# The mix of a four-layer network: head steps in another order, two operations on other engines, the next layer's first transfers in its tail

## What is computed

```python
x  = x + s * g                       # layer 1's result, then:
xn = layernorm(x)
# mixer of layer 2 (8 chunks of 2 sequences x 256 tokens, width 128):
h        = layernorm(xn) * ln_g + ln_b
xi, z    = split(h @ W_in)
xc       = silu(causal_conv4(xi) + conv_b)
dt, B, C = split(xc @ W_xp)
delta    = softplus(dt @ W_dt + dt_bias)
state_t  = state_{t-1} * exp(delta_t * A) + delta_t * xc_t * B_t     # 256 channels x 16 states
y        = sum_n(state * C) + xc * D_skip
s        = (y * silu(z)) @ W_out + xn
# gate of layer 2: 16 experts, 2 per token, 128 -> 512 -> 128 with relu
g        = silu(sum over the two experts of weight * (relu(xn @ W1 + b1) @ W2 + b2))
x        = x + s * g                 # layer 3 begins with this
```

## Time and profile before

| | us |
|---|---|
| median of 3 runs | 3733.08 (3729.55 to 3736.5) |
| the profiled execution | 3726.74 |
| its span, first to last instruction | 3725.0 |
| first to last scan of the mix (128 scans) | 1253.4 to 1972.7 |
| busy: PE 2920.9, DVE 2268.6, ACT 1773.6, POOL 1190.1 | |
| granted TensorE clock, mean over the span | 0.901 |

### The profile page before, as it was taken

One profiled execution on the slowest core, in us unless ns is written; L12 is line 12 of the kernel. 1 busy time (PEld: TensorE's weight loads), 2 busy tenths in 40 slices (PEclk: granted clock), 3 DMA queues, 4 the chain that ended last, 5 costly groups with the idle time before them and its releaser, 6 DMA issues. The chain is left out here.

```text
span 3725.0 us, 54922 instructions
## 1 busy us (share of the span) xinstructions
PE 2920.9 (78%) x20472; PEld 1596.2 (43%) x20580; DVE 2268.6 (61%) x3194; ACT 1773.6 (48%) x3989; POOL 1190.1 (32%) x854
## 2 busy tenths in 40 slices
PE   5887888888624788888876888888888888888887
PEld 3444444444323234444442444444544444444443
DVE  3444444544347678788784666675757656675755
ACT  2334333443223455555552554645555554645555
POOL 0000000000134355555453534343443534443432
PEclk9888998999855899999987999999999998999989
DMA  2000000000022233333231000000000000000000
GB/s 108 9 8 6 3 8 8 6 3 8 30 97 88 59 85 84 84 85 88 81 93 47 10 4 10 6 3 12 3 13 4 13 4 10 7 4 10 3 4 4
DMA packets 82485, 112.67 MB, mean 30 GB/s; under 512 B 9952, under 2 KB 47328, under 8 KB 81632
## 3 DMA queue, kind: packets, MB, share of 16 engines
q1 hardware_dynamic: 76896, 98.83, 8.8%
q0 software_dynamic: 5376, 11.02, 1.1%
HBM read 82.55 MB, written 27.26 MB: 29 GB/s over the span
## 5 line engine op out<-in xcount | busy, mean ns | idle before, releaser
L1470 POOL TENSOR_TENSOR l2m_ST<-l2m_ST,l_CT 128x1024 f32<-128x1024 f32 x128 | 316.3, 2471 | 353.0 <-DVE l2m_ST L1413 353.0
L394 ACT ACTIVATE l_PT<-PB 128x512 f32<-128x512 f32 x512 | 277.9, 595 | 315.8 <-PE PB L292 315.8
L1413 DVE TENSOR_TENSOR_SCAN l2m_ST<-l2m_DA,l2m_DB 128x1024 f32<-128x1024 f32 x128 | 354.0, 2766 | 4.4
L436 DVE TENSOR_REDUCE keep_MXP<-PB 128x4 f32<-128x1024 f32 x256 | 301.1, 1218 | 61.4 <-PE PB L265 61.4
L292 PE MATMUL PB<-l_QM,l_KP 32*128 32x256 f32 x2048 | 283.1, 394 | 55.7 <-ACT l_PT L394 55.7
L731 POOL MEMSET l_KV<- 128x4 f32 x8 | 0.8, 104 | 854.5 <-POOLq L109 854.5
L1868 POOL TENSOR_TENSOR l_PT<-l_PT,ahead_PEN 128x512 f32<-128x512 f32 x176 | 232.7, 1353 | 63.5 <-ACT l_PT L394 63.0
L292 PEld LDWEIGHTS PB<-l_QM,l_KP 32*128 32x128 f32 x2048 | 188.0, 188 | 134.4 <-ACT l_PT L394 87.8
L1407 DVE TENSOR_TENSOR l2m_DB<-PB,l_BT 128x1024 f32<-128x1024 f32 x128 | 155.4, 1214 | 139.5 <-PE PB L1252 139.3
L1358 ACT ACTIVATE l2m_DA<-PB,keep_aneg 128x510 f32<-128x510 f32 x256 | 161.0, 683 | 162.8 <-DVE l2m_ST L1413 89.4
L2063 ACT ACTIVATE l3f_PP<-PB,l3f_MN 128x128 f32<-128x128 f32 x512 | 180.8, 372 | 118.8 <-DVE l3f_MN L2129 118.8
(11 more groups left out here) (463 smaller groups left out, 6393.2 us busy)
## 6 DMA issues: line engine op xcount, KB each, us to landing
l2m_WB<-in_w2f_dram SPq DMA_DIRECT2D x80, 320.0 KB, 3.0
l2m_WB<-in_w2f_dram SPq DMA_DIRECT2D x80, 258.0 KB, 2.7
l2m_XR<-xs_mid SPq DMA_DIRECT2D x80, 64.0 KB, 1.8
ys_mid<-l2m_YO SPq DMA_DIRECT2D x80, 64.0 KB, 2.8
s_mid<-keep_S SPq DMA_DIRECT2D x18, 256.0 KB, 2.1
w3fs<-in_w3f_dram SPq DMA_DIRECT2D x1, 3127.0 KB, 18.6
x_mid<-keep_X SPq DMA_DIRECT2D x10, 256.0 KB, 3.0
keep_XI<-in_x_dram SPq DMA_DIRECT2D x9, 256.0 KB, 3.0
```

The costliest lines, as they stand in the source:

```text
L394: nc.scalar.activation(b.PT[:, u % slots].rearrange("p k q -> p (k q)"), PB[:, 4 + u % STBANKS, :], ACT.Exp).then_inc(s.exp_done, 1)
L436: nc.vector.tensor_reduce(dst[:, 2 * pair:2 * pair + 2, :, 16 + n % 2], PB[:, 2 * pair:2 * pair + 2, :].rearrange("p r (t k) -> p r t k", ...
L1413: nc.vector.tensor_tensor_scan(b.ST[:, g % RING].rearrange("p k t -> p (k t)"), b.DA[:, g % 2].rearrange("p k t -> p (k t)"), b.DB[:, g % ...
L1470: nc.gpsimd.tensor_tensor(b.ST[:, g % RING], b.ST[:, g % RING], b.CT[:, k % 2, :].unsqueeze(1).broadcast_to([128, 2, T]), ALU.mult).then_i ...
```

## The change

1. In the mix the projection moves from step 2 to step 3 on TensorE, and the sum with the input from step 3 to step 4 on VectorE (`add_input` stands behind that step's scan).
2. The head's steps 8 to 13 move one step later, to 9 to 14 (`head_step`). Step 8 has no head.
3. The affine step of the head's normalisation moves from VectorE (L927) to ScalarE. The subtraction L933 moves from VectorE to GpSimd, behind its multiplication of step 13, and VectorE's L934 waits for it; `drives` of the next chunk moves behind the multiplication of step 14. For chunk 0 the same happens at the end of the router's block.
4. The block behind the mix goes. SP issues its two loads ahead of the last sum's store. GpSimd copies the places at its start, and behind the last multiplication waits for all tile stores, issues two gathers, does the last gating, and issues the other six.

```diff
+    elif step == 2:
+        act.wait_ge(s.xm_scaled, k + 1)
+        XS = b.XM[:, :, TAPS - 1:]
+        nc.scalar.activation(XS, XS, ACT.Identity, scale=w.g, bias=w.b).then_inc(s.xm_ready, 1)
...
+def head_step(n):
+    return n if n < 8 else n - 1 if n > 8 else None
+
+
+def head_pool(nc, pool, s, b, k):
+    pool.wait_ge(s.dt_log, k + 1)
+    nc.gpsimd.tensor_tensor(b.EE[:], b.UU[:], b.EE[:], ALU.subtract).then_inc(s.error_taken, 1)
...
-        link(nc.vector.scalar_tensor_tensor(out=XS, in0=seq(PB[:, LANE, :]), scalar=-0.5, in1=seq(u), op0=ALU.mult, op1=ALU.mult))
-        nc.vector.tensor_scalar(XS, XS, w.g, w.b, ALU.mult, ALU.add).then_inc(s.xm_ready, 1)
+        nc.vector.scalar_tensor_tensor(out=XS, in0=seq(PB[:, LANE, :]), scalar=-0.5, in1=seq(u), op0=ALU.mult, op1=ALU.mult).then_inc(s.xm_scaled, 1)
...
     elif step == 13:
-        dve.wait_ge(s.dt_log, k + 1)
-        link(nc.vector.tensor_tensor(b.EE[:], b.UU[:], b.EE[:], ALU.subtract))
+        dve.wait_ge(s.error_taken, k + 1)
...
+                head_pool(nc, pool, mix, head, 0)
                 pool.wait_ge(s.scattered0, 16 * TT * CHUNKS)
...
                 store_tile(TILES - 1)
+                sp.wait_ge(s.s_stored, 16)
+                load_gated(nc, sp, c, 0, x_mid, s_mid, s.first_loaded)
                 store_sum(CHUNKS - 1)
+                sp.wait_ge(s.first_loaded, 32)
...
-                        if n == 2 and k:
+                        if n == 3 and k:
                             project(k - 1)
                         if k + 1 < CHUNKS:
-                            head_tensor(nc, pe, s, c, w, b, PB, k + 1, n)
+                            head_tensor(nc, pe, s, c, w, b, PB, k + 1, head_step(n))
...
-                        if k and n == 3:
+                        if k and n == 4:
                             add_input(k - 1)
...
+                nc.gpsimd.tensor_copy(r.places[:], r.idx[:, :, 0:TT]).then_inc(s.places_copied, 1)
                 drives(0)
...
                         if n == 13 and k + 1 < CHUNKS:
+                            head_pool(nc, pool, s, b, k + 1)
+                        if n == 14 and k + 1 < CHUNKS:
                             drives(k + 1)
+                rows = [(a, t) for a in range(2) for t in range(TT)]
+                pool.wait_ge(s.places_copied, 1)
+                pool.wait_ge(s.tile_stored0, 8 * TILES)
+                pool.wait_ge(s.tile_stored1, 8 * TILES)
+                for a, t in rows[:2]:
+                    gather_tile(nc, pool, c, r, ys_mid, a, t, s.gathered)
                 gated(CHUNKS - 1, 1)
-        clear(nc, s)
+                for a, t in rows[2:]:
+                    gather_tile(nc, pool, c, r, ys_mid, a, t, s.gathered)
+                pool.wait_ge(s.gathered, 32 * TT)
+        clear(nc, s, soft)
...
-        with ExitStack() as io:
-            s = record(**semaphores(nc, io, "first_loaded places_copied")._asdict(), gathered=soft.soft0)
-            with nc.Block() as block:
...
-                    load_gated(nc, sp, c, 0, x_mid, s_mid, s.first_loaded)
-                    sp.wait_ge(s.first_loaded, 32)
...
-                    gather_mixed(nc, pool, c, r2, ys_mid, s.gathered)
-                    pool.wait_ge(s.gathered, 32 * TT)
-            clear(nc, s, soft)
```

More of the change, by code:

```diff
@@ L778 @@
             "taps_ready xm_ready xz_ready z_copied conv_ready x_copied silu_x xd_ready bc_copied dt_ready dt_raw dt_u dt_error dt_log delta_ready drive_ready "
-            "b_spread b_copied c_spread c_copied pads_set gaps_set delta_spread drive_spread decay_ready drive_done state_ready part_ready y_added "
+            "b_spread b_copied c_spread c_copied pads_set gaps_set places_copied first_loaded xm_scaled error_taken delta_spread drive_spread decay_ready drive_done state_ready part_ready y_added "
             "y_taken y_gated mamba_ready s_added ")
@@ L1188, in layer2_route, with layer2_mix @@
         clear(nc, s, soft)
-def layer2_mix(nc, c, w, wf, r, s, head, xn_mid, s_mid, xs_mid, ys_mid, PB):
+def layer2_mix(nc, c, w, wf, r, s, soft, head, x_mid, xn_mid, s_mid, xs_mid, ys_mid, PB):
     with ExitStack() as ctx:
+        s = record(**s._asdict(), gathered=soft.soft0)
         b = buffers(nc, ctx, "l2m", DU=[2, 2, T], DA=[2, 2, T], DB=[2, 2, T], ST=[RING, 2, T],
@@ L1393, in _ @@
                         if k + 1 < CHUNKS:
-                            head_scalar(nc, act, s, c, w, b, PB, link, k + 1, n)
+                            head_scalar(nc, act, s, c, w, b, PB, link, k + 1, head_step(n))
             @block.vector
@@ L1436, in _ @@
                         drive(k, n)
-                        if k and n == 3:
+                        if k and n == 4:
                             add_input(k - 1)
                         if k + 1 < CHUNKS:
-                            head_vector(nc, dve, s, c, w, b, PB, link, k + 1, n)
+                            head_vector(nc, dve, s, c, w, b, PB, link, k + 1, head_step(n))
                 take_sums(CHUNKS - 1, 1)
@@ L2332, in network @@
             layer2_route(nc, c, v2, r2, soft, mix, head, x_mid, s_mid, y_mid, xn_mid, xs_mid, PB)
-            layer2_mix(nc, c, v2, w2f, r2, mix, head, xn_mid, s_mid, xs_mid, ys_mid, PB)
-        with ExitStack() as io:
-            s = record(**semaphores(nc, io, "first_loaded places_copied")._asdict(), gathered=soft.soft0)
-            with nc.Block() as block:
-                @block.sync
-                def _(sp):
-                    load_gated(nc, sp, c, 0, x_mid, s_mid, s.first_loaded)
-                    sp.wait_ge(s.first_loaded, 32)
[L2342 to L2345, removed]
-                    gather_mixed(nc, pool, c, r2, ys_mid, s.gathered)
-                    pool.wait_ge(s.gathered, 32 * TT)
-            clear(nc, s, soft)
+            layer2_mix(nc, c, v2, w2f, r2, mix, soft, head, x_mid, xn_mid, s_mid, xs_mid, ys_mid, PB)
         h = buffers(nc, ctx, "ahead", X=[T], XN=[T], PEN=[TT, SEQ], GA=[T + TT], GU=[T + TT], AJ=[T], PJ=[T], T1=[TT, SEQ], T2=[TT, SEQ],
```

## The result

The changed kernel takes 3764.15 us (median of 20 runs, 3756.26 to 3808.6), the kernel before, run beside it 20 times, 3738.47. The ratio is 1.0097 with a 95% interval of 1.0073 to 1.012: slower by 1%, which is some 36 us. The forecast was slower by 0.4% (+15 us, 3748).

A forecast was written before the change was run, and what follows sets the result against it. No engine was full; scans (VectorE) and multiplications (GpSimd) exclude each other, with TensorE pacing some steps. Chunks 1 to 6 +21.9, chunk 0 +3.4, chunk 7 -1.2, router +1.3, tail -10.5: +15 us, 3748 us; range 3718 to 3766.

The forecast's parts named there:

- the forecast one: Main case for the whole kernel: slower by 0.4%, +15 us, 3748 us; chance 0.40.
- the term for the low clock: Full chunks: new TensorE idle before L1309 and in step 8 brings 1.2 GHz, 1.5 us each; +2.0 us per chunk.
- Part 1: Steps 2 to 5: scan 3 starts 3.8 us earlier, but the sum behind scan 4 delays L1309; -1.3 us per chunk.
- Part 2: Steps 8 to 12, widths a step later: step 8 -0.9, step 9 +0.9, step 11 -0.3, step 12 +1.2; +0.9 us per chunk.
- Part 3: Steps 13 to 15: step 13 shortens 2.15, step 14's serial chain adds 3.5, step 15 adds 0.7; +2.05 us per chunk.
- rival (c): Step 14: scan 14 starts before the subtraction, which then waits 2.3 us; slower still, 3759 us; chance 0.14.
- (b): Rival: step 14's chain is hidden, the subtraction fits before scan 14; with a high clock -13 us, 3720 us; chance 0.22.
- Chunk 7: Last chunk, without a head: projection and sum changes -2.0, clock +0.8; -1.2 us.
- Router: Chunk 0's head in the router's block: subtraction 2.35 for 1.20 us and a hand-over twice; +1.3 us.
- Tail: Gathers and loads moved into the mix's end, one barrier fewer: -10.5 us, at worst -8.

The follow-up runs named there:

- the filler: Changed kernel plus matmuls into an unread bank, filling TensorE's three idle stretches (steps 5, 8 and 14): ratio 1.0029, chunk 94.0 us.

## Why the prediction was wrong

The sign was right, the case was the forecast one (no rival's mechanism appears), and the size forecast, +15 us, was less than half of the 36 that the ratio gives; the medians differ by 26, the traces by 34 from the first scan on. What failed is the term for the low clock, and by some 4 us the one for the router's hand-over. By its steps:

- **Part 1, -1.3**: -1.6 with the filler (22.4 for 24.0, of which the kernel before spent part at half the clock, too). The chain is as told: 6.3 to scan 3 (forecast 6.4), 14.07 to the expert product (14.1), idle from the turning of the rows until then. Right.
- **Part 2, +0.9**: +0.4 with the filler. Steps 8, 9, 11 and 12 gave -1.7, +1.1, -0.3 and +1.2 (forecast -0.9, +0.9, -0.3, +1.2); of the -1.7, 0.8 is the low clock that the mean of before held; without it the part costs +1.2. Right.
- **Part 3, +2.05**: +2.5 with the filler, whose step 13 took 6.6 where the changed kernel has 5.9 (forecast 5.7). Steps 14 and 15 were 7.8 and 5.1 (forecast 8.0 and 5.3). The scan did start inside the subtraction's time and wait, so rival (c) didn't come and neither did the hidden chain of (b). Right.
- **The low clock, +2.0 per chunk**: this is the step that failed. It measured 4.4 against the filler. Part of that the kernel before had paid already: its low stretch in step 8 came in three of seven chunks (1, 3 and 6: 9.35, 9.07 and 9.07 us, for 7.56 in the others), not in the two that the prediction counted, which is 0.8 per chunk and not 0.4. So what compares with +2.0 is +3.6, and the forecast's own bounds ended at 2.6. In chunk 0 it was +10 (102.5 for 92.5), where the term allowed 0.9. Two more things in it were wrong. The price of 1.5 us at step 8 was read from L842 (3.29 for 1.92), which was only one of the operations in a low stretch; the stretch after step 8's idle time is 6.83 us long and costs step 9 9.9 for 6.9, 3.0 us. The second place, step 5, cost 1.3 (8.67 for 7.35), about as priced. A third place was not listed at all: part 3 keeps TensorE waiting for the widths, and the 10.24 us at half clock behind that cost 0.9 in step 14 and 0.9 in step 15. Step 0 gives back 1.1 (3.44 for 4.58). Steps 12 and 13 are 1.0 longer with the filler, by the low stretches that this kernel met there, so that the sum is 1.3 + 3.3 (steps 8 and 9) - 1.0 + 1.9 - 1.1 = 4.4.
- **Chunk 7, -1.2**: -4.0. With no head in step 2 scan 3 comes 3.9 us after scan 2 (9.9 before), not 6.4, and steps 3 to 5 give only 3.2 of the 6.0 back: -2.8. The other 1.1 is step 0, the giving back of chunk 6's last steps. The term took the full chunk's figure for scan 3.
- **Router, +1.3**: +5.6 from the logarithm to the first scan (15.60 for 9.96). In all six kernels with the subtraction on GpSimd it is 15.60, in the eight others 9.8 to 11.8. The chain itself cost the 1.2 forecast; the term put nothing for the later start of the mix's block (4.90 us after the widths, 2.0 to 3.0 in the others) and for the first spread at half the clock. Why the block starts later was not tested.
- **Tail, -10.5**: -10.4. Right.

Sum over the mix in the traces: 6 x 5.8 + 13.5 - 4.0 = +44.3 (forecast +24.1), of which the low clock has 6 x 3.6 + 10 = 32 where the forecast had 14. That is 18 of the 20 us by which the mix's forecast was short. The filler kernel is at 1.0029 (1.0 to 1.0059); the forecast without its clock term was +1 us, at the lower end of that.

What takes back the gain of part 1 is, as forecast, the sum behind scan 4: `add_input` in step 4 costs 3.1 us per chunk (95.3 against 98.4) in the changed kernel and 4.0 with the head unshifted (88.4 against 92.4), each with what the low clock adds there. Why the low stretches in one place change length when another is filled was not settled, and what the filler itself costs was not measured. Not tried was a bank of its own for the projection, so that the first expert product need not wait for the sum.

## What to carry over

An idle time of TensorE is priced by what TensorE does after it, and for as long as the low stretch lasts, not by the operation that follows it: list every new idle time that a reordering makes, also those inside a chain that was forecast for another reason. A producer moved later needs its consumer's place looked at as well: here the projection in step 3 is worth 4 us per chunk if the sum stays in step 3 (88.4 for 92.6), and nothing if the sum goes behind the next scan. Before moving work between two engines that exclude each other, ask what is in series with it: the same subtraction on GpSimd cost 1.6 us in step 13 and, with the head a step later, saved 1.6 in step 14 (0.7 over steps 13 to 15).

## What was not expected of the hardware

- TensorE's clock fell to its lower level (0.50, 1.2 GHz) behind idle times of 1.86 and 0.76 us with one small matmul between them, and stayed there for 6.83 us while TensorE was busy for 6.57 of them. In chunk 0 one such stretch (from 1367.54) lasted 10.24 us with TensorE busy throughout. Around the idle time of 3.98 us it was low for 10.24 (TensorE busy for 9.11 of them), around that of 2.82 us for 3.41. The same length of idle time doesn't always have the same effect: 1.85 us in step 8 of the kernel before was followed by the low level in three of seven chunks, in the kernel with the subtraction alone on GpSimd in six of seven. The Trainium skill (TensorE: Matmul & The Clock Gate, The HAM clock gate) says that an idle engine is set to 1.2 GHz and that activity releases it. The trace agrees with the direction. How short the idle times were that the low level followed (step 8 in all seven chunks, 2.78 to 2.82 us ahead of the expert product in chunks 1 to 5, but not 2.39 us there in chunk 6), and how long it outlasted the return to work, the rows showed.
- The exclusion of VectorE and GpSimd also decides who goes next. In the changed kernel scan 14 asked 0.5 us after the subtraction had begun and ran as soon as it had ended (3.99 long), while the multiplication behind it waited for L945 (3.23 for 2.35). The Trainium skill (SBUF — State Buffer, Who interferes with whom) names the order of issue, and the two rows agree.
- Two gathers from GpSimd, the second of them beside VectorE's sums (L1436, which reads PSUM, from 2065.11) for its last 0.39 us, took 1.03 and 0.95 us, the same as those with VectorE idle.
